# Splitting the w2t loads of the first stage in two, and waiting for each x tile by itself

## The chip, the cores and the metric

The program runs on the 8 cores of one Trainium2 chip. Each core gets 1024 of the 8192 rows of the input and all of the weights; no core talks to another. The metric is the device time of the slowest core, in microseconds.

## The reference, cut to what matters

```python
def reference(x, w1, w2, b2, sparse_mask, qweight, scales, scaled_zeros, bias):
    def attn(x):                      # D = 4096
        a = jnp.einsum('ds,td->st', w1, w2) * sparse_mask
        y = jnp.einsum('bds,st->bdt', x, a) + b2
        return gelu(y)                # exact gelu
    def ffn(x):
        w = (qweight.astype(f32) * scales + scaled_zeros).reshape(4096, 4096)
        return jnp.einsum('bsi,oi->bso', x, w) + bias
    x = x + 0.5 * ffn(layernorm(x))
    x = x + attn(layernorm(x))
    x = x + 0.5 * ffn(layernorm(x))
    return x
```

x is 8192 x 4096 in float32. The mask is a band: of 32 x 8 blocks of 128 x 512 it touches 55.

## The kernel before

There are two blocks, one after the other. **The first block** makes the weights, on each core for itself. It builds the masked product of w1 and w2 (`amat`, bf16, in DRAM) for the 55 blocks that the mask touches, and it turns the quantized weight into a transposed bf16 matrix (`wdqT`, in DRAM). **The second block** does the three layers for the core's 1024 rows, 512 rows at a time (u = 0 and 1), in three passes each (p = 0, 1, 2: ffn, attention, ffn).

In the first block the order is written out by hand. `P_PAIRS` holds 14 pairs (sb, tc): sb is one of four blocks of 1024 columns of w1 (`w1blk`, 128 x 32 x 1024 in bf16), tc one of eight blocks of 512 columns of w2 (`w2t`, two slots of 128 x 32 x 512 in bf16, slot qq % 2). A pair has 1 to 6 tiles k (`K_TILES`), 55 in all; the pairs have 6, 5, 2, 2, 5, 6, 1, 2, 6, 6, 2, 1, 6 and 5 tiles. A tile is 32 matmuls of 128 x 128 by 128 x 512 (L393, dc = 0 to 31) into one of two PSUM tiles `pa`. VectorE multiplies it by the mask (L314, `aev`), GpSimd stores it (L256, `amat`).

Where a tc comes for the first time (`TC_FIRST`, 8 pairs: 0, 1, 2, 5, 6, 9, 10, 13), GpSimd loads w2t from w2T in float32 with a cast to bf16 (L247, semaphore `wt_ld`), and ScalarE's queue writes it back as `w2b` (L348). Where a tc comes again (6 pairs: 3, 4, 7, 8, 11, 12), SP's queue loads it from `w2b` (L273, `wr_ld`). Both loads stand in their queues behind what the pair before issues: L247 comes after the last amat store of the pair before, L273 after its last mask load. Pairs 3, 7 and 11 begin a new sb: GpSimd also loads w1blk in four parts (L234), the first two counted on `w1_lda`, the last two on `w1_ldb`. TensorE waits for `w1_lda` ahead of the first matmul of such a pair and for `w1_ldb` ahead of the 17th:

```python
                            for dc in range(NC):
                                if new_sb and k == PAIR_TILES[qq][0] and dc == 16:
                                    t.wait_ge(w1_ldb, 32 * (sb + 1))
```

Between the tiles the quantized weight is worked on by fixed positions: GpSimd loads rows (`qt`, L224), VectorE dequantizes (`wout`, L302, 32 instructions a row block), TensorE transposes (L372, 32), VectorE copies out (`asm`, L326, 32), and ScalarE's queue stores (`wdqT`, L357).

In the second block a pass begins with a layer norm of four row tiles j. For the first pass ScalarE sums x (L496) and its squares (L503), VectorE forms the scale and normalizes (L616), TensorE transposes 32 blocks (L539), VectorE copies them out (L627, `hT`). When all four are through, eight groups of matmuls (L559) run on weights that SP loads (L465, L453, `mv`, two slots) and VectorE adds the result to `x_sb` (L641). After u = 0, SP stores the four tiles of `x_sb` (L474, a semaphore `st_o[j]` each) and then issues the first two mv loads of u = 1. GpSimd waits for each store and loads the next rows into the same tile:

```python
                    for j in range(NT):
                        g.wait_ge(st_o[j], 16)
                        g.dma_start(
                            out=x_sb[:, j * D:(j + 1) * D],
                            in_=x_in[512 + j * 128:512 + (j + 1) * 128, :],
                        ).then_inc(x_ld2, 16)
```

ScalarE waits ahead of its first L496 of u = 1 until `x_ld2` stands at 64, that is for all four.

Of the kernel before, what the change touches and what calls it, by code (L numbers as in the profile page):

```python
# [15 lines left out]
NC = 32  # L16
# [101 lines left out]
def build_nc():  # L118
# [47 lines left out]
    wt_ld = semn("wt_ld", 2)  # L166
    wr_ld = semn("wr_ld", 2)
    mk_ld = semn("mk_ld", 2)
    p1_st = semn("p1_st", 2)
    x_ld = sem1("x_ld")  # L170
    x_ld2 = sem1("x_ld2")
    st_o = semn("st_o", 4)
    mv_ld = semn("mv_ld", 2)

    with es:
# [7 lines left out]
        with nc.Block() as block:  # L183
            from contextlib import ExitStack as _ES

            with _ES() as es_1:
# [15 lines left out]
                def _(g):  # L202
# [25 lines left out]
                    for qq, (sb, tc) in enumerate(P_PAIRS):  # L228
# [12 lines left out]
                        if TC_FIRST[qq]:  # L241
                            if qq >= 2:
                                g.wait_ge(p1_pe, K_BEFORE[qq - 1])
                                if TC_FIRST[qq - 2]:
                                    g.wait_ge(wb_st[P_PAIRS[qq - 2][1]], 16)
                            sl2 = (qq % 2) * NC * 512
                            g.dma_start(  # L247
                                out=w2t[:, sl2:sl2 + NC * 512]
                                    .rearrange("p (c t) -> p c t", t=512),
                                in_=w2T.rearrange("(c p) t -> p c t", p=128)  # L250
                                    [:, :, tc * 512:(tc + 1) * 512],
                            ).then_inc(wt_ld[qq % 2], 16)
                        for k in PAIR_TILES[qq]:
                            Sg = K_TILES[k][3]
# [10 lines left out]
                def _(sync):  # L265
                    for qq, (sb, tc) in enumerate(P_PAIRS):
                        if not TC_FIRST[qq]:
                            sync.wait_ge(p1_pe, K_BEFORE[qq - 1])
                            if TC_FIRST[qq - 2]:
                                sync.wait_ge(wb_st[P_PAIRS[qq - 2][1]], 16)  # L270
                            sync.wait_ge(wb_st[tc], 16)
                            sl2 = (qq % 2) * NC * 512
                            sync.dma_start(  # L273
                                out=w2t[:, sl2:sl2 + NC * 512]
                                    .rearrange("p (c t) -> p c t", t=512),
                                in_=w2b.rearrange("(c p) t -> p c t", p=128)
                                    [:, :, tc * 512:(tc + 1) * 512],
                            ).then_inc(wr_ld[qq % 2], 16)
                        for k in PAIR_TILES[qq]:
                            Sg = K_TILES[k][3]  # L280
# [54 lines left out]
                def _(s):  # L335
# [6 lines left out]
                    for _, kind, idx in sorted(acts):  # L342
                        if kind == 0:
                            qq = idx
                            tc = P_PAIRS[qq][1]
                            sl2 = (qq % 2) * NC * 512
                            s.wait_ge(wt_ld[qq % 2], WT_CNT[qq])
                            s.dma_start(  # L348
                                out=w2b.rearrange("(c p) t -> p c t", p=128)
# [14 lines left out]
                def _(t):  # L364
# [12 lines left out]
                    for qq, (sb, tc) in enumerate(P_PAIRS):  # L377
# [8 lines left out]
                        for k in PAIR_TILES[qq]:  # L386
# [3 lines left out]
                            for dc in range(NC):  # L390
                                if new_sb and k == PAIR_TILES[qq][0] and dc == 16:
                                    t.wait_ge(w1_ldb, 32 * (sb + 1))
                                ins = t.matmul(  # L393
# [11 lines left out]
            with _ES() as es_2:  # L405
# [12 lines left out]
                def _(g):  # L418
                    for j in range(NT):
                        g.wait_ge(st_o[j], 16)  # L420
                        g.dma_start(
                            out=x_sb[:, j * D:(j + 1) * D],
                            in_=x_in[512 + j * 128:512 + (j + 1) * 128, :],
                        ).then_inc(x_ld2, 16)

# [57 lines left out]
                def _(s):  # L483
                    for _tc in range(8):
                        s.wait_ge(wb_st[_tc], 16)
                    for u in range(2):
                        for p in range(3):
                            for j in range(NT):
# [3 lines left out]
                                if p == 0:  # L492
                                    s.wait_ge(x_ld if u == 0 else x_ld2, 64)
                                    if u == 1:
# [183 lines left out]
```

## Time and profile before

| what | us |
|---|---|
| runs: median of 2 (lowest, highest) | 3102.33 (3054.62, 3150.04) |
| the profiled execution | 3068.76 |
| its span, slowest core (core 3) | 3067.2 |
| spans of the other cores | 3022.0 to 3050.6 |
| granted TensorE clock, mean, share of full | 0.761 to 0.768 |
| first block, to the issue of the first x load | 1377.3 |
| PE busy in the whole span | 1889.1 |
| PE L393 busy (1760 matmuls) | 458.8 |

The profiled execution is one run of its own beside the two that make the median. The span runs from the first to the last instruction of the slowest core; 1.6 us lie around it. A line such as L393 is a line of the kernel before. "Idle before" is time in which an engine stood still ahead of an instruction, and the name behind the arrow is what ended it.

### The profile page before, as it was taken

The page shows a single profiled execution, that of the slowest core. Times are in us where ns is not written, and L with a number is a line of the kernel's source. Part 1 is how long each engine was busy: PE and PEld are TensorE (multiplying, and loading weights), DVE is VectorE, ACT ScalarE, POOL GpSimd, SP SyncE. Part 2 cuts the span into 40 slices and gives each one's busy share as a digit, 9 for nine tenths or more (in the row PEclk, how much of TensorE's full clock was granted, in tenths as well). Part 3 has the DMA queues.
Part 4 walks back from the last instruction along what each step waited for, and adds up shares of the span by engine and source line. Part 5 has one row for each costly group of instructions (what it writes and reads, how often), then busy time and mean ns, then how long its engine had stood idle before and what let it go on. Part 6 is the DMA issues. An engine that isn't in the chain of part 4 may idle for free.

```text
span 3067.2 us, 25494 instructions; the slowest of 8 cores (3022.0 to 3067.2 us)
## 1 busy us (share of the span) xinstructions
PE 1889.1 (62%) x8280; PEld 845.1 (28%) x8280; DVE 757.6 (25%) x3395; ACT 168.3 (5%) x157; POOL 83.0 (3%) x124
## 2 busy tenths in 40 slices
PE   0552254721657225372999765889629997658896
PEld 0220122300223112131343322333213333224332
DVE  0032234420454224354000324100031003241000
ACT  0000000000000000004000213000040002130000
POOL 1000000000000000000000000000000000000000
PEclk9965677855778657685899776889758997668888
DMA  9688979999588996866233014144372430141342
GB/s 157 144 164 174 174 132 139 172 178 180 117 142 179 187 181 122 148 137 214 96 124 110 23 50 132 55 138 136 93 236 82 137 110 23 50 132 55 130 145 110
DMA packets 402702, 399.49 MB, mean 130 GB/s; under 512 B 135696, under 2 KB 370992, under 8 KB 396432
## 3 DMA queue, kind: packets, MB, share of 16 engines
q1 hardware_dynamic: 180240, 213.39, 23.9%
q0 software_dynamic: 57856, 117.37, 23.8%
q10 hardware_dynamic: 164480, 67.11, 9.5%
q8 instruction: 72, 1.18, 0.2%
q14 instruction: 54, 0.44, 0.1%
HBM read 407.47 MB, written 91.10 MB: 163 GB/s over the span
## 4 chain that ended last, share of the span: by engine, by line
PE 54%; another core or an unknown queue 17%; DVE 12%; DMA 8%; issue 5%; ACT 2%; DVEq 1%; POOL 0%; SPq 0%; ACTq 0%; POOLq 0%
PE ps L559 36%; PE pa L393 13%; DMA w2t<-w2T 5%; DVE x_sb L641 3%; DVE asm L326 3%; DVE hT L627 2%; PE ptr L372 2%; DVE wout L302 2%; DVE h_tmp L616 2%; PE ps L569 2%; PE tr L539 1%; DMA x_sb<-x_in 1%; DMA y_out<-x_sb 1%; ACT sq_scr L503 1%
## 5 line engine op out<-in xcount | busy, mean ns | idle before, releaser
L559 PE MATMUL ps<-mv,hT 128*128 128x512 bf16 x4536 | 1098.7, 408 | 141.9 <-DVE x_sb L641 137.4
L393 PE MATMUL pa<-w2t,w1blk 128*128 128x512 bf16 x1760 | 458.8, 428 | 702.6 <-DMA w2t<-w2T 449.8
L559 PEld LDWEIGHTS ps<-mv,hT 128*128 128x128 bf16 x4536 | 466.6, 104 | 772.2 <-issue 312.8
L393 PEld LDWEIGHTS pa<-w2t,w1blk 128*128 128x128 bf16 x1760 | 186.3, 108 | 961.7 <-issue 805.0
L641 DVE SCALAR_TENSOR_TENSOR x_sb<-ps,x_sb 128x512 f32<-128x512 f32 x128 | 80.8, 687 | 1007.0 <-PE ps L569 1007.0
L539 PE MATMUL tr<-ident_bf,h_tmp 128*128 128x128 bf16 x768 | 132.8, 264 | 257.6 <-DVE h_tmp L616 245.5
L314 DVE TENSOR_TENSOR aev<-pa,mkt 128x512 bf16<-128x512 f32 x55 | 37.9, 690 | 838.8 <-PE pa L393 838.8
L302 DVE TENSOR_SCALAR wout<-qt,scl_sb,zro_sb 128x128 bf16<-128x128 bf16 x1024 | 235.5, 325 | 0.0
L372 PE MATMUL ptr<-ident_bf,wout 128*128 128x128 bf16 x1024 | 161.2, 230 | 53.8 <-DVE asm L326 43.4
L326 DVE COPY asm<-ptr 128x128 bf16<-128x128 bf16 x1024 | 166.5, 219 | 18.2 <-PE ptr L372 3.7
L539 PEld LDWEIGHTS tr<-ident_bf,h_tmp 128*128 128x128 bf16 x768 | 80.2, 105 | 311.7 <-issue 291.7
L627 DVE COPY hT<-tr 128x128 bf16<-128x128 bf16 x768 | 125.0, 220 | 34.3 <-PE tr L539 18.5
L372 PEld LDWEIGHTS ptr<-ident_bf,wout 128*128 128x128 bf16 x1024 | 97.9, 98 | 121.6 <-issue 81.6
L503 ACT ACTIVATE sq_scr<-x_sb 128x4096 bf16<-128x4096 f32 x24 | 86.8, 3616 | 563.2 <-DVE x_sb L641 560.5
L641 DVE SCALAR_TENSOR_TENSOR x_sb<-gel,x_sb 128x512 f32<-128x512 f32 x64 | 41.8, 690 | 172.7 <-ACT gel L521 172.7
L496 ACT ACT_TABLE_LOAD x1 | 1.3, 1283 | 1406.2 <-DMA x_sb<-x_in 1406.2
L256 POOL DMA_DIRECT2D amat<-aev x55 | 30.3, 551 | 1255.3 <-DVE aev L314 887.7
L616 DVE TENSOR_SCALAR h_tmp<-x_sb,stats 128x4096 bf16<-128x4096 f32 x24 | 57.9, 2412 | 4.6 <-DVE stats L611 4.6
L496 ACT ACTIVATE sq_scr<-x_sb 128x4096 bf16<-128x4096 f32 x8 | 28.9, 3617 | 335.7 <-DMA x_sb<-x_in 334.7
L521 ACT ACTIVATE gel<-ps 128x512 f32<-128x512 f32 x64 | 36.4, 596 | 156.2 <-PE ps L569 149.1
L596 DVE TENSOR_SCALAR stats<-stats 128x1 f32<-128x1 f32 x24 | 3.6, 151 | 119.6 <-ACT sq_scr L503 118.3
L569 PE MATMUL ps<-fb_bf,halves_bf 1*128 1x512 bf16 x128 | 33.0, 377 | 0.0
(32 smaller groups left out, 134.0 us busy)
## 6 DMA issues: line engine op xcount, KB each, us to landing
mv<-wdqT SPq DMA_DIRECT2D x32, 4096.0 KB, 15.0
w1blk<-w POOLq DMA_DIRECT2D x16, 2048.0 KB, 57.3
w2t<-w2T POOLq DMA_DIRECT2D x8, 4096.0 KB, 49.4
w2b<-w2t ACTq DMA_DIRECT2D x8, 4096.0 KB, 16.9
qt<-qw POOLq DMA_DIRECT2D x32, 1024.0 KB, 12.8
wdqT<-asm ACTq DMA_DIRECT2D x32, 1024.0 KB, 11.2
w2t<-w2b SPq DMA_DIRECT2D x6, 4096.0 KB, 67.0
y_out<-x_sb SPq DMA_DIRECT2D x8, 2048.0 KB, 16.0
```

The source lines that it names most:

```text
L302: v.tensor_scalar(wout[:, sl * D + gg * 128: sl * D + gg * 128 + 128], qt[:, sl * D + gg * 128: sl * D + gg * 128 + 128], scl_sb[:, r * 32 ...
L314: v.tensor_tensor(aev[:, (k % 2) * 512:(k % 2) * 512 + 512], pa[k % 2][:], mkt[:, (k % 2) * 512:(k % 2) * 512 + 512], op=ALU.mult,).then_i ...
L326: v.tensor_copy(asm2[:, (r % 2) * D + blk * 128: (r % 2) * D + blk * 128 + 128], ptr[b % 4][:],).then_inc(wqev, 1)
L372: t.transpose(ptr[b % 4][:], wout[:, (r % 2) * D + blk * 128: (r % 2) * D + blk * 128 + 128], ident_bf[:]).then_inc(wqtr, 1)
L393: ins = t.matmul(pa[k % 2][:], w1blk[:, dc * 1024 + st * 128: dc * 1024 + st * 128 + 128], w2t[:, (qq % 2) * NC * 512 + dc * 512: (qq % 2) ...
L503: s.activation(sq_scr[:], x_sb[:, j * D:(j + 1) * D], AF.Square, accum_out=stats[:, 4 + j:5 + j]).then_inc(ac_ln, 1)
L539: t.transpose(trp[tg % 4][:], h_tmp[:, ic * 128:(ic + 1) * 128], ident_bf[:]).then_inc(p2_tr, 1)
L559: t.matmul(psb[j][:], hT[:, ic * 512 + j * 128: ic * 512 + j * 128 + 128], mv[:, sl + ii * 512:sl + ii * 512 + 512], start=(ii == 0), stop ...
L569: ins = t.matmul(psb[j][:], lrow[0:1, :], brow[0:1, oc * 512:(oc + 1) * 512], start=False, stop=True,)
L616: v.tensor_scalar(h_tmp[:], x_sb[:, j * D:(j + 1) * D], stats[:, 8 + j:9 + j], stats[:, 20 + j:21 + j], op0=ALU.subtract, op1=ALU.mult).th ...
L627: v.tensor_copy(hT[:, ic * 512 + j * 128: ic * 512 + j * 128 + 128], trp[tg % 4][:],).then_inc(p2_trv, 1)
L641: v.scalar_tensor_tensor(x_sb[:, j * D + oc * 512: j * D + oc * 512 + 512], src, 1.0, x_sb[:, j * D + oc * 512: j * D + oc * 512 + 512], o ...
```

## The change

Each of the 14 w2t loads becomes two: chunks 0 to 15 on the semaphore it had, chunks 16 to 31 on a new one (`wtb_ld` for GpSimd's loads, `wrb_ld` for SP's). TensorE waits for the second one ahead of the 17th matmul of a pair's first tile. ScalarE's queue waits for both ahead of the write-back. Apart from that the four x loads of u = 1 get a semaphore each, and ScalarE waits ahead of L496 of tile j for the load of tile j.

```diff
+    wtb_ld = semn("wtb_ld", 2)
+    wrb_ld = semn("wrb_ld", 2)
-    x_ld2 = sem1("x_ld2")
+    x_l2 = semn("x_l2", 4)
...
+                            w2Tv = w2T.rearrange("(c p) t -> p c t", p=128)
                             g.dma_start(
-                                out=w2t[:, sl2:sl2 + NC * 512]
+                                out=w2t[:, sl2:sl2 + 16 * 512]
                                     .rearrange("p (c t) -> p c t", t=512),
-                                in_=w2T.rearrange("(c p) t -> p c t", p=128)
-                                    [:, :, tc * 512:(tc + 1) * 512],
+                                in_=w2Tv[:, 0:16, tc * 512:(tc + 1) * 512],
                             ).then_inc(wt_ld[qq % 2], 16)
+                            g.dma_start(
+                                out=w2t[:, sl2 + 16 * 512:sl2 + NC * 512]
+                                    .rearrange("p (c t) -> p c t", t=512),
+                                in_=w2Tv[:, 16:NC, tc * 512:(tc + 1) * 512],
+                            ).then_inc(wtb_ld[qq % 2], 16)
...
                             s.wait_ge(wt_ld[qq % 2], WT_CNT[qq])
+                            s.wait_ge(wtb_ld[qq % 2], WT_CNT[qq])
...
                             for dc in range(NC):
-                                if new_sb and k == PAIR_TILES[qq][0] and dc == 16:
-                                    t.wait_ge(w1_ldb, 32 * (sb + 1))
+                                if k == PAIR_TILES[qq][0] and dc == 16:
+                                    if new_sb:
+                                        t.wait_ge(w1_ldb, 32 * (sb + 1))
+                                    t.wait_ge(
+                                        (wtb_ld if TC_FIRST[qq] else wrb_ld)
+                                        [qq % 2], WT_CNT[qq])
...
-                        ).then_inc(x_ld2, 16)
+                        ).then_inc(x_l2[j], 16)
...
                                 if p == 0:
-                                    s.wait_ge(x_ld if u == 0 else x_ld2, 64)
+                                    if u == 0:
+                                        s.wait_ge(x_ld, 64)
+                                    else:
+                                        s.wait_ge(x_l2[j], 16)
                                     if u == 1:
                                         s.wait_ge(p2_ev, 96)
```

SP's load from `w2b` is split in the same way, on `wr_ld` and `wrb_ld`. The tables `P_PAIRS`, `QW_AT`, `DQ_AT` and `TR_AT` are as before.

On TensorE the tiles of pair 1 stand so before (the first row is the pair's first matmul, L393):

```order
L393 MATMUL pa<-w2t,w1blk 128x512 [waits wt_ld1,p1_ev]
L393 MATMUL pa<-w2t,w1blk 128x512 x31
L393 MATMUL pa<-w2t,w1blk 128x512 [waits p1_ev]
L393 MATMUL pa<-w2t,w1blk 128x512 x31
L393 MATMUL pa<-w2t,w1blk 128x512 [waits p1_ev]
```

and so now (L410 is the same line in the changed kernel):

```order
L410 MATMUL pa<-w2t,w1blk 128x512 [waits wt_ld1,p1_ev]
L410 MATMUL pa<-w2t,w1blk 128x512 x15
L410 MATMUL pa<-w2t,w1blk 128x512 [waits wtb_ld1]
L410 MATMUL pa<-w2t,w1blk 128x512 x15
L410 MATMUL pa<-w2t,w1blk 128x512 [waits p1_ev]
```

The first tile has a second wait in its middle; the matmuls keep their order. On GpSimd's queue the load of pair 2 stood, ahead of the w1blk loads of pair 3, so:

```order
L247 DMA w2t<-w2T 128x32x512 [waits p1_pe,wb_st0]
L256 DMA amat<-aev 128x512 [waits p1_ev]
L224 DMA qt<-qw 128x4096 [waits q_dq]
L256 DMA amat<-aev 128x512 [waits p1_ev]
L234 DMA w1blk<-w 128x8x1024 [waits p1_pe]
```

and stands now so:

```order
L250 DMA w2t<-w2T 128x16x512 [waits p1_pe,wb_st0]
L255 DMA w2t<-w2T 128x16x512
L263 DMA amat<-aev 128x512 [waits p1_ev]
L226 DMA qt<-qw 128x4096 [waits q_dq]
L263 DMA amat<-aev 128x512 [waits p1_ev]
L236 DMA w1blk<-w 128x8x1024 [waits p1_pe]
```

The second half follows the first at once; nothing else has changed its place.

## Rows read from the trace of the kernel before

**Rows 1.** The page, section 4: shares of the span in the chain, by line.

```profile
PE ps L559 36%; PE pa L393 13%; DMA w2t<-w2T 5%; DVE x_sb L641 3%; DVE asm L326 3%; DVE hT L627 2%; PE ptr L372 2%; DVE wout L302 2%; DVE h_tmp L616 2%; PE ps L569 2%; PE tr L539 1%; DMA x_sb<-x_in 1%; DMA y_out<-x_sb 1%; ACT sq_scr L503 1%
```

**Rows 2.** Waits up to 1400 us: us in total, times, longest us.

```profile
PE pa L393 <- DMA w2t<-w2T: 449.8, 8, 96.3
...
PE pa L393 <- DMA w1blk<-w: 252.9, 6, 57.9
```

**Rows 3.** Timeline of PE: start us, us, what [idle before <-releaser].

```profile
96.27 43.63 PE L393 MATMUL pa<-w2t,w1blk 128*128 128x512 bf16 x192 [96.27 <-DMA w2t<-w2T]
...
299.95 9.64 PE L393 MATMUL pa<-w2t,w1blk 128*128 128x512 bf16 x32 [58.35 <-DMA w2t<-w2T]
...
386.85 5.42 PE L393 MATMUL pa<-w2t,w1blk 128*128 128x512 bf16 x16 [56.15 <-DMA w1blk<-w]
420.77 12.43 PE L393 MATMUL pa<-w2t,w1blk 128*128 128x512 bf16 x48 [28.50 <-DMA w1blk<-w]
...
546.84 9.09 PE L393 MATMUL pa<-w2t,w1blk 128*128 128x512 bf16 x32 [44.80 <-DMA w2t<-w2T]
...
791.00 6.42 PE L393 MATMUL pa<-w2t,w1blk 128*128 128x512 bf16 x16 [29.82 <-DMA w1blk<-w]
...
929.44 8.94 PE L393 MATMUL pa<-w2t,w1blk 128*128 128x512 bf16 x32 [41.78 <-DMA w2t<-w2T]
```

**Rows 4.** Timeline of POOL: three groups of load issues.

```profile
142.57 1.71 POOL L247 DMA_DIRECT2D w2t<-w2T  x1
...
326.59 3.52 POOL L234 DMA_DIRECT2D w1blk<-w  x4 [0.29 <-issue]
...
504.56 1.77 POOL L247 DMA_DIRECT2D w2t<-w2T  x1
```

**Rows 5.** The four w1blk loads issued at 326.6: issue to landing.

```profile
DMA to landing us min/median/max: 37.1/67.2/91.4
```

**Rows 6.** Windows: length, PE, PEld, DVE, ACT, POOL busy, PEclk, DMA share, GB/s.

```profile
110.00:120.00 10.00, 10.00 (x48) 4.56 (x47) 1.27 (x2) 0.00 (x0) 0.56 (x1) 1.00 0.28 80
...
300.00:310.00 10.00, 9.82 (x36) 3.89 (x36) 0.16 (x1) 0.00 (x0) 0.00 (x0) 0.74 0.97 322
320.00:330.00 10.00, 8.69 (x50) 4.56 (x48) 4.95 (x28) 0.00 (x0) 3.96 (x5) 0.95 1.06 143
...
1000.00:1010.00 10.00, 4.39 (x21) 1.77 (x19) 9.57 (x39) 0.00 (x0) 2.83 (x3) 0.92 0.59 126
```

**Rows 7.** Timeline between the halves: ACT's 1st, 2nd and 4th L496, PE's first L559.

```profile
2254.52 3.62 ACT L496 ACTIVATE sq_scr<-x_sb 128x4096 bf16<-128x4096 f32 x1 [334.65 <-DMA x_sb<-x_in]
...
2263.41 3.62 ACT L496 ACTIVATE sq_scr<-x_sb 128x4096 bf16<-128x4096 f32 x1 [0.20 <-ACT stats L509]
...
2284.73 3.62 ACT L496 ACTIVATE sq_scr<-x_sb 128x4096 bf16<-128x4096 f32 x1 [0.20 <-ACT stats L509]
...
2305.11 1.44 PE L559 MATMUL ps<-mv,hT 128*128 128x512 bf16 x3 [0.69 <-DVE hT L627]
```

**Rows 8.** Line L421, first of its four loads: issue and landing.

```profile
L421 POOL DMA_DIRECT2D x_sb<-x_in x1: 542/542/542, 2208.6 to 2208.6; - x1
...
DMA to landing us min/median/max: 20.4/20.4/20.4
```

**Rows 9.** Line L421, second of its four loads.

```profile
L421 POOL DMA_DIRECT2D x_sb<-x_in x1: 539/539/539, 2217.6 to 2217.6; - x1
...
DMA to landing us min/median/max: 21.7/21.7/21.7
```

**Rows 10.** DMA issues of SP at 2203: KB each, us to landing.

```profile
mv<-wdqT SPq DMA_DIRECT2D x1, 4096.0 KB, 66.7
```

**Rows 11.** Core 2, the same place: first load of L421, first L496.

```profile
L421 POOL DMA_DIRECT2D x_sb<-x_in x1: 539/539/539, 2199.4 to 2199.4; - x1
...
DMA to landing us min/median/max: 20.3/20.3/20.3
...
2248.91 3.62 ACT L496 ACTIVATE sq_scr<-x_sb 128x4096 bf16<-128x4096 f32 x1 [335.85 <-DMA x_sb<-x_in]
```

More of the change, by code:

```diff
@@ L272, in _ @@
                             sl2 = (qq % 2) * NC * 512
+                            w2bv = w2b.rearrange("(c p) t -> p c t", p=128)
                             sync.dma_start(
-                                out=w2t[:, sl2:sl2 + NC * 512]
+                                out=w2t[:, sl2:sl2 + 16 * 512]
                                     .rearrange("p (c t) -> p c t", t=512),
-                                in_=w2b.rearrange("(c p) t -> p c t", p=128)
-                                    [:, :, tc * 512:(tc + 1) * 512],
+                                in_=w2bv[:, 0:16, tc * 512:(tc + 1) * 512],
                             ).then_inc(wr_ld[qq % 2], 16)
+                            sync.dma_start(
+                                out=w2t[:, sl2 + 16 * 512:sl2 + NC * 512]
+                                    .rearrange("p (c t) -> p c t", t=512),
+                                in_=w2bv[:, 16:NC, tc * 512:(tc + 1) * 512],
+                            ).then_inc(wrb_ld[qq % 2], 16)
                         for k in PAIR_TILES[qq]:
```

## Prediction

> **What bounds the kernel now.** I read the page's chain first. Its largest part is the second block's matmuls, L559 with 36%, which the change does not touch; w2t loads stand in it with 5%, and the two transfers of x between the halves with about 1% each [rows 1]. So the change can only work at two places, and I looked at each.
>
> The first is the first block. The table of waits up to 1400 us says that TensorE stood 449.8 us for a w2t load from w2T, in 8 waits, and 252.9 us for w1blk, in 6 [rows 2]. Eight is the number of pairs with a new tc; the six others are the two waits each of pairs 3, 7 and 11. No wait for a load from w2b is in the table: the six loads of SP are never late. The timeline of TensorE shows the pattern: a stand of 41 to 58 us, then a first tile of 32 matmuls in 8.9 to 9.6 us [rows 3]. GpSimd issues such a load only when the pair before is through, at 142.57 for pair 1 and 504.56 for pair 5 [rows 4], and pair 5 starts 42.3 us after its issue, at 546.84. So load and computation follow one another and do not overlap, and what shortens the computation behind a landing brings the next issue forward.
>
> The second place lies between the halves. The first x load is issued at 2208.6 and lands 20.4 us later [rows 8]; ScalarE's first L496 starts at 2254.52 and is said to wait for an x load [rows 7], though the tile that it reads has been there for 25 us. It waits for all four.
>
> **The w2t loads, eight pairs.** Take a load that lands at T. Before, 32 matmuls of the first tile stand behind T; now 16, since the first 16 run when the first half has landed. For this the halves must land one after the other with at least the time of 16 matmuls between. The four w1blk loads show that they do: they are issued within 3.5 us on the same queue [rows 4], the earliest lands after 37.1 us and the latest after 91.4 [rows 5], and TensorE began on the first two at 386.85 and on the last two at 420.77 [rows 3]. Two of four had landed after 60 of 94 us, or 64%. The same share of a 42 us load is 27 us, which leaves 15 us; 16 matmuls after a stand take 5.42 [rows 3]. They fit.
>
> What is gained is not these 5.42. After the second wait the array is slow again: the 48 matmuls from 420.77 take 12.43 us, although 16 had run 28.5 us earlier, while 192 in a row take 43.63, or 0.227 each [rows 3]. So the slow start is paid twice, and what is saved is 32 matmuls after a stand (9.64, 9.09, 8.94; mean 9.22) less 16 after a stand (5.42; once 6.42). That is 3.8, or 2.8 by the slower row; 16 matmuls at 0.227 are 3.6. I take 3.7, with 2.8 and 4.2 as ends (9.64 less 5.42).
>
> The Trainium skill has the rule behind this (TensorE: Matmul & The Clock Gate, "What's actually happening"): an idle array falls back to 1.2 GHz, so work put ahead of an idle stretch warms nothing behind it. The trace agrees, with 5.42 us for 16 after a stand against 3.6 in a long run. Without that rule one would book 9.22 less 3.6, 5.6 a pair.
>
> How much of 3.7 reaches the end depends on what the DMA engines do behind the landing. In long pairs they run dry before the next issue: their share is 0.28 at 110 us, 0.59 at 1000 us [rows 6]. There the next load starts earlier, and all of it counts: pairs 0, 1, 5, 9 and 13, 5 x 3.7 = 18.5. Pairs 2, 6 and 10 have only 1 or 2 tiles, and the next wait is for w1blk, issued at 326.59 behind pair 2 [rows 4]. From the landing at 299.95 to that issue the engines are full, with shares of 0.97 and 1.06 [rows 6]: write-back, wdqT stores and weight rows are on their way. An issue 3.7 us earlier takes bandwidth from those, and they then take it back. The gain lies between 0 and 3.7; for something under half the bandwidth I take 1.5, 3 x 1.5 = 4.5.
>
> Twice the issues cost GpSimd nothing: four w1blk issues take 3.52 us, 0.88 each, and a whole w2t issue 1.71 to 1.77 [rows 4]; two halves make the same. SP's split loads are not waited for now, and the same bytes move in the same order, so they cost nothing unless halves move slower (below). ScalarE's write-back waits for both halves, which is when it was issued before. The evictions, dequantization and transposes of a pair keep their order and shift with the first tile.
>
> **The x tiles.** ScalarE can begin at 2208.6 + 20.4 = 2229.0 instead of 2254.5: 25.4 us, with the 0.1 of a semaphore taken off. From there to TensorE's first L559 it took 50.6 us (2254.52 to 2305.11) [rows 7], and this is work of four engines that the loads only have to feed in time. The second load lands at 2217.6 + 21.7 = 2239.3 [rows 9]; ScalarE would want it at 2263.41 less 25.4, 2238.0, so it is 1.3 late. The fourth is wanted at 2284.73 less 25.4 = 2259.3, and all have landed by 2254.5 [rows 7]. The 1.3 counts in full if ScalarE sets the pace and not at all if VectorE does; I take 0.5, which leaves 24.9. Next comes the first mv load: issued at 2203 it lands after 66.7 us [rows 10], at 2269.7, and is wanted at 2305.1 less 25.4 = 2279.7. It has 10 us to spare, so it covers nothing. On core 2 the same gap is 2199.4 + 20.3 to 2248.9 [rows 11], 29.2 us, the upper end; with 1.3 lost and a landing 4 us later than here, 20 is the lower.
>
> **The sum.** 18.5 + 4.5 + 24.9 = 47.9 us. The profiled execution took 3068.8 (span 3067.2 and 1.6 around it), so 3020.9, or 1.6% less; I say 3021. The two other runs stand at 3054.6 and 3150.0, with a median of 3102.3 that lies between two far ends; the profiled one is near the lower, and the forecast is for such an execution. A measurement of this kernel can tell about 2% from no change, and the forecast lies inside that.
>
> **The rivals.**
> 1. The DMA engines give more back. Pairs 2, 6 and 10 bring nothing, and the long pairs lose some too, since qt loads and wdqT stores are paced by computation and pile up when it is shorter. For: shares near 1 after a landing. Against: 0.28 and 0.59 before the next issue [rows 6]. With 2 us a long pair: 10 + 24.9 = 35, so 3034.
> 2. The split does not do what it says: both halves land within a few us, since each of the engines finishes at its own time. Then TensorE waits as before, and only the x tiles count: 3044. Against it stand the w1blk landings [rows 5].
> 3. Slower: halves move at a lower rate than the whole. Place: the 449.8 + 252.9 = 702.7 us in which TensorE waits for loads [rows 2]. Each 1% of rate costs 7.0 us; from 6.8% on the whole gain is gone, and at 10% it is 3068.8 - 47.9 + 70.3 = 3091. For it: nothing in the trace shows this load in halves. Against: w1blk is loaded in quarters already, with the engines at 1.06 in the window of its issue [rows 6].
> 4. More: each of the eight gives 4.2 and the x tiles 29.2 as on core 2. 33.6 + 29.2 = 62.8, so 3006, just over 2%.
>
> The Trainium skill (DMA: Bandwidth & Descriptors, "Anatomy of one DMA") gives each DMA a fixed cost of about 2.0 us, mostly the wait for the write's receipt. If the eight awaited loads each paid it once more, that would be an estimate of 16 us and 3037. No row here isolates it, and the second half is queued before the first has ended, so I leave it out.
>
> **How the numbers follow.** The forecast gets 0.58, rival 1 0.13, rival 2 0.08, rival 3 0.07, rival 4 0.14. The range goes down to rival 4 on an execution like the fastest (3006 less the 14.1 by which 3054.6 lies under 3068.8, about 2992), rounded to 2990. Upward it takes in rivals 1 and 2 with the same scatter above 3044 and the lower third of rival 3: 3068. Faster by over 2% needs 3007 or less against 3068.8: rival 4 and the scatter below the forecast, 0.27. Slower by over 2% needs rival 3 with 16% less rate, 0.04. Within 2%: 0.69.
>
> **What would show it.** L410 (the old L393) must show eight pairs of waits, the first ended by a w2t load some 15 us before the second, with 16 matmuls of about 5.4 us between. The w2t waits in all must fall from 449.8 by less than the early matmuls; from the issue of pair 5 to its second landing must stay 42 us. The first block must end near 1354 instead of 1377. ScalarE's first L496 must begin 20 us after the first x load's issue, with L559 51 us behind. I am wrong if the second half lands later than the whole did, if the w1blk waits grow by more than 3.7 us a pair, or if mv becomes the wait ahead of L559.

## The result, and the profile after

The changed kernel is faster. Its median is 2988.2 us (2977.7 to 3005.9, 11 runs), beside 3058.4 us for before in the same measurement, and the ratio is 0.9777 with a 95% interval of 0.9749 to 0.9806. Measured twice more (c1 and c3 below) the ratio is 0.9834 (0.9797 to 0.9871) and 0.9873 (0.9807 to 0.9939). The forecast was 3021 us, or 1.6% less; measured are 2.2%, 1.7% and 1.3%. Whether it is "faster by over 2%" or "within 2%" stays undecided: the first interval lies almost wholly below 0.98, the second almost wholly and the third wholly above. Executions in which one die ran at a lower clock are left out of the ratios.

The page of the changed kernel is taken on core 4. Line L410 is the old L393, L438 the old L421, L516 the old L496. The waits up to 1400 us, us in total, times, longest:

```profile
PE pa L410 <- DMA w2t<-w2T: 384.0, 16, 87.5
...
PE pa L410 <- DMA w1blk<-w: 248.4, 6, 52.7
```

The waits for w2T are 16 instead of 8, as they must be, and 384 us instead of 450 [rows 2]; those for w1blk have hardly moved. Where a pair starts is seen in the timeline of TensorE, for pair 5 (start us, us, what, idle before):

```profile
509.85 6.35 PE L410 MATMUL pa<-w2t,w1blk 128*128 128x512 bf16 x16 [26.29 <-DMA w2t<-w2T]
523.11 1.01 PE L410 MATMUL pa<-w2t,w1blk 128*128 128x512 bf16 x2 [6.91 <-DMA w2t<-w2T]
524.34 5.31 PE L410 MATMUL pa<-w2t,w1blk 128*128 128x512 bf16 x13 [0.22 <-issue]
```

and in that of GpSimd, the two issues of the same load:

```profile
486.09 1.21 POOL L250 DMA_DIRECT2D w2t<-w2T  x1
487.29 1.17 POOL L255 DMA_DIRECT2D w2t<-w2T  x1
```

The first half lands 23.8 us after its issue, the second 13.3 us behind it; between them 16 matmuls take 6.35 us and TensorE stands for 6.91. Behind the second landing 16 matmuls are left (one has no record), and they take 6.5 us: the slow start is paid again. Before, this place read 9.09 for 32 [rows 3].

Between the halves of the rows, in the timeline of core 4:

```profile
2151.18 0.54 POOL L438 DMA_DIRECT2D x_sb<-x_in  x1 [835.90 <-DMA y_out<-x_sb]
...
2173.73 3.62 ACT L516 ACTIVATE sq_scr<-x_sb 128x4096 bf16<-128x4096 f32 x1 [309.86 <-DMA x_sb<-x_in]
...
2184.38 3.62 ACT L516 ACTIVATE sq_scr<-x_sb 128x4096 bf16<-128x4096 f32 x1 [1.97 <-DMA x_sb<-x_in]
...
2204.14 3.62 ACT L516 ACTIVATE sq_scr<-x_sb 128x4096 bf16<-128x4096 f32 x1 [0.48 <-ACT stats L529]
...
2224.30 11.08 PE L579 MATMUL ps<-mv,hT 128*128 128x512 bf16 x40 [1.07 <-DVE hT L647]
```

ScalarE starts 22.6 us after the first issue, where it was 45.9 [rows 7, 8]. The second tile's load is late by 1.97 us, as forecast (1.3), and TensorE's first L579 stands 50.6 us behind ScalarE's start, to the tenth as before. On this core the lateness was hidden by the rest of the chain; on the others that distance is 50.4 to 51.6 us now, where it was 50.4 to 50.8. The first mv load landed after 67.0 us, 10 us ahead of its use.

### The profile page after: what moved, and what is told of

The parts are those of the page before. It is cut to its first block, busy times and chain, and to the rows that moved or that the text cites. A ratio compares the mean times of both kernels' runs of the same rounds, so it can differ in the third digit from the quotient of the medians.

```text
span 2990.9 us, 25381 instructions; the slowest of 8 cores (2958.5 to 2990.9 us)
## 1 busy us (share of the span) xinstructions
PE 1887.0 (63%) x8131; PEld 847.9 (28%) x8280; DVE 754.0 (25%) x3395; ACT 168.4 (6%) x157; POOL 88.4 (3%) x132
## 3 DMA queue, kind: packets, MB, share of 16 engines
q0 software_dynamic: 57984, 117.37, 24.9%
## 4 chain that ended last, share of the span: by engine, by line
PE 54%; DMA 13%; DVE 13%; another core or an unknown queue 10%; issue 6%; ACT 2%; DVEq 1%; POOL 0%; ACTq 0%; SPq 0%; POOLq 0%
PE ps L579 36%; PE pa L410 13%; DMA w2t<-w2T 9%; DVE asm L338 3%; DVE x_sb L661 3%; DVE hT L647 2%; DVE wout L314 2%; PE tr L559 2%; DVE h_tmp L636 2%; DMA x_sb<-x_in 2%; DMA w1blk<-w 2%; PE ps L589 2%; PE ptr L385 1%; ACT sq_scr L523 1%
## 5 line engine op out<-in xcount | busy, mean ns | idle before, releaser
L579 PE MATMUL ps<-mv,hT 128*128 128x512 bf16 x4438 | 1085.6, 407 | 150.8 <-DVE x_sb L661 137.1
L410 PE MATMUL pa<-w2t,w1blk 128*128 128x512 bf16 x1709 | 470.6, 440 | 641.5 <-DMA w2t<-w2T 384.0
L579 PEld LDWEIGHTS ps<-mv,hT 128*128 128x128 bf16 x4536 | 465.8, 103 | 768.8 <-issue 306.8
L410 PEld LDWEIGHTS pa<-w2t,w1blk 128*128 128x128 bf16 x1760 | 190.8, 110 | 909.7 <-issue 767.4
L559 PE MATMUL tr<-ident_bf,h_tmp 128*128 128x128 bf16 x768 | 131.6, 265 | 231.3 <-DVE h_tmp L636 218.4
L385 PE MATMUL ptr<-ident_bf,wout 128*128 128x128 bf16 x1024 | 159.8, 228 | 54.4 <-DVE asm L338 43.6
L559 PEld LDWEIGHTS tr<-ident_bf,h_tmp 128*128 128x128 bf16 x768 | 79.8, 104 | 284.6 <-issue 265.3
L516 ACT ACTIVATE sq_scr<-x_sb 128x4096 bf16<-128x4096 f32 x8 | 28.9, 3617 | 313.0 <-DMA x_sb<-x_in 311.8
L438 POOL DMA_DIRECT2D x_sb<-x_in x4 | 2.4, 594 | 867.7 <-DMA y_out<-x_sb 867.7
```

The lines of the kernel that those rows point to most:

```text
L385: t.transpose(ptr[b % 4][:], wout[:, (r % 2) * D + blk * 128: (r % 2) * D + blk * 128 + 128], ident_bf[:]).then_inc(wqtr, 1)
L410: ins = t.matmul(pa[k % 2][:], w1blk[:, dc * 1024 + st * 128: dc * 1024 + st * 128 + 128], w2t[:, (qq % 2) * NC * 512 + dc * 512: (qq % 2) ...
L559: t.transpose(trp[tg % 4][:], h_tmp[:, ic * 128:(ic + 1) * 128], ident_bf[:]).then_inc(p2_tr, 1)
L579: t.matmul(psb[j][:], hT[:, ic * 512 + j * 128: ic * 512 + j * 128 + 128], mv[:, sl + ii * 512:sl + ii * 512 + 512], start=(ii == 0), stop ...
```

## The experiments

Twelve runs were made, in four series; each series has its own runs of before beside it, on the same chip (one chip for e1 to e8, c1 and c2, another for e9 and c3; for the first measurement the chip is not on record). The ratios rest on 4 to 11 executions of the run, that of e6 on two. To read the first block I took two spans from the timelines of GpSimd and TensorE for each of its 11 load-bound stretches (the eight w2T loads and the w1blk loads of pairs 3, 7 and 11), as means over the 8 cores: from the load's issue to TensorE's last start on it ("to the landing"), and from there to the next such issue ("computation"). The first stretch begins at 0. They add up to the issue of the first x load.

| run | ratio (95%) | landings, sum | computation, sum | first x load | second block |
|---|---|---|---|---|---|
| before, first trace | | 694.8 | 660.0 | 1354.9 | 1687.1 |
| changed, first trace | 0.9777 (0.9749 to 0.9806) | 681.1 | 635.0 | 1316.1 | 1661.2 |
| e1 x tiles only | 0.9929 (0.9885 to 0.9972) | 672.6 | 663.5 | 1336.1 | 1649.8 |
| e2 w2t loads only | 0.9925 (0.9876 to 0.9975) | 668.5 | 638.1 | 1306.6 | 1686.4 |
| e3 both halves awaited | 1.0027 (0.9991 to 1.0062) | 672.7 | 667.7 | 1340.4 | 1683.6 |
| e4 SP's loads whole | 0.9945 (0.9904 to 0.9986) | 677.2 | 651.7 | 1328.9 | 1682.7 |
| c1 changed, again | 0.9834 (0.9797 to 0.9871) | 673.4 | 636.7 | 1310.1 | 1647.2 |
| c2 before, again | 0.9994 (0.9969 to 1.0020) | 671.7 | 663.3 | 1335.0 | 1678.4 |
| e5 pieces of 24 and 8 | 0.9744 (0.9710 to 0.9778) | | | 1283.5 | 1656.1 |
| e6 loads ahead, whole | 0.9585 (0.9544 to 0.9626) | | | | |
| e7 filled stand | 0.9796 (0.9745 to 0.9847) | | | 1299.5 | |
| e8 loads ahead, half | 0.9589 (0.9516 to 0.9662) | | | | 1656.9 |
| c3 changed, third time | 0.9873 (0.9807 to 0.9939) | 668.3 | 637.2 | 1305.5 | 1654.8 |

The second block is the span less the first x load's issue. A block's mean over the cores is steadier than the slowest core, but it is one execution each.

**What had to be explained.** Comparing the two first traces, the first block was 39 us shorter, not 23, and 13.7 of it came from loads that landed sooner. The prediction has no such term. Is it the split, or the execution?

**e1_x_only**: the kernel before with this edit alone.

```diff
-                        ).then_inc(x_ld2, 16)
+                        ).then_inc(x_l2[j], 16)
...
-                                    s.wait_ge(x_ld if u == 0 else x_ld2, 64)
+                                    if u == 0:
+                                        s.wait_ge(x_ld, 64)
+                                    else:
+                                        s.wait_ge(x_l2[j], 16)
```

> Only the four semaphores of the x loads, the w2t loads whole as before. My step: 25 us less between the halves (a ratio of 0.992), and a first block as long as before (first x load issued on average over the cores at 1355 us). Rival, that part of the extra gain sits behind the first block: more than 35 us less.

Measured: 0.9929, 22 us. It fits the 25, and its interval reaches from 8 to 35 us. The rival, over 35, is out. What was not expected is the first block: 1336 instead of 1355 us, though nothing in it is changed.

**e2_w2_only**: the changed kernel with the edit of e1 taken back.

```diff
-                        ).then_inc(x_l2[j], 16)
+                        ).then_inc(x_ld2, 16)
...
-                                    if u == 0:
-                                        s.wait_ge(x_ld, 64)
-                                    else:
-                                        s.wait_ge(x_l2[j], 16)
+                                    s.wait_ge(x_ld if u == 0 else x_ld2, 64)
```

> Only the split w2t loads, x tiles awaited together as before. The whole change gave 0.978, some 68 us; if the two parts add up, this one gives 40 to 45 us (0.986), of which 25 are matmuls that run ahead of the second landing and 14 are landings that come sooner. By the sum of the prediction it would be 23 us (0.9925).

Measured: 0.9925, 23 us, on the number of the prediction and below the 40 that the first comparison had led me to expect. Against e1's trace the computation is 25.4 us shorter and the landings are 4.1. The interval, 8 to 38 us, leaves out the 40 to 45 and does not part 23 from 30.

**e3_no_early**: e2 with the early start taken out.

```diff
                         if TC_FIRST[qq]:
                             t.wait_ge(wt_ld[qq % 2], WT_CNT[qq])
+                            t.wait_ge(wtb_ld[qq % 2], WT_CNT[qq])
                         else:
                             t.wait_ge(wr_ld[qq % 2], WT_CNT[qq])
+                            t.wait_ge(wrb_ld[qq % 2], WT_CNT[qq])
...
-                                if k == PAIR_TILES[qq][0] and dc == 16:
-                                    if new_sb:
-                                        t.wait_ge(w1_ldb, 32 * (sb + 1))
-                                    t.wait_ge(
-                                        (wtb_ld if TC_FIRST[qq] else wrb_ld)
-                                        [qq % 2], WT_CNT[qq])
+                                if new_sb and k == PAIR_TILES[qq][0] and dc == 16:
+                                    t.wait_ge(w1_ldb, 32 * (sb + 1))
```

> All w2t loads split, x tiles awaited together as before, but TensorE waits for both halves ahead of the first matmul, so nothing runs ahead. Theory A, that a load in two pieces lands sooner as a whole by itself: about 14 us less than before (0.995), with the mean time from the issue of a w2T load to TensorE's start near 38 us for pairs 1, 5, 9 and 13. Theory B, that the landings come sooner only because less other traffic is left once the matmuls are ahead: no gain, within 5 us of before, and that time stays near 40 to 43 us.

Measured: 1.0027. The landings of pairs 1, 5, 9 and 13 came after 38.4, 37.2, 37.7 and 37.0 us, as theory A says, but the kernel gained nothing, and e1, with whole loads, has 38.6, 37.4, 37.6 and 36.3. So neither theory holds: the landings are at 36 to 39 us in every trace of this series, whole or split. It also prices the split itself: 14 more transfers, with nothing started early, cost between nothing and 19 us by the interval, and the landings' sum differs from e1's by 0.1 us.

**e4_sp_whole**: e2 with SP's load in one piece.

```diff
-                            sync.dma_start(
-                                out=w2t[:, sl2:sl2 + 16 * 512]
...
-                            ).then_inc(wr_ld[qq % 2], 16)
-                            sync.dma_start(
-                                out=w2t[:, sl2 + 16 * 512:sl2 + NC * 512]
...
-                            ).then_inc(wrb_ld[qq % 2], 16)
+                            sync.dma_start(
+                                out=w2t[:, sl2:sl2 + NC * 512]
...
+                            ).then_inc(wr_ld[qq % 2], 16)
...
-                                    t.wait_ge(
-                                        (wtb_ld if TC_FIRST[qq] else wrb_ld)
-                                        [qq % 2], WT_CNT[qq])
+                                    if TC_FIRST[qq]:
+                                        t.wait_ge(wtb_ld[qq % 2], WT_CNT[qq])
```

> GpSimd's w2T loads split, SP's loads from w2b whole again, x tiles awaited together as before. Theory A1, that what lands sooner is GpSimd's own load because it is cut: as e2, 40 to 45 us less than before. Theory A2, that it is the cut of SP's loads, which share the DMA engines with pairs 2, 6, 10 and with w1blk: 10 us or more short of e2. By the prediction SP's cut is worth nothing.

Measured: 0.9945, 17 us, with an interval (4 to 29 us) that covers e2's 23. SP's cut is worth nothing that these runs can show. In the trace the computation is 13.6 us longer than e2's, but its cores had a lower granted clock, 0.750 to 0.767 in the mean of the span where e2's had 0.759 to 0.772. Pair 0, which no load of SP can touch, shows it: on cores 0 to 3 its computation took 48.8 to 49.7 us (granted 0.81 from 110 to 140 us on core 0), on cores 4 to 7 42.0 to 43.3 us (1.00 on core 4), where e2 has 42.1 to 43.6 on all eight. So the 13.6 us cannot be put down to SP's cut.

**c1_after and c2_before**: the two kernels themselves, unedited, on one chip.

> The changed kernel again, on a chip on which the two parts are run too. If the parts add up, 0.985 to 0.986 (0.9929 times 0.9925), 44 us, which is close to the forecast. If whole and parts differ for a reason of their own (the parts help each other), 0.978 as at first, 68 us.

> The kernel before as a control, for its trace. On the first trace of before the w2T loads of pairs 1, 5, 9, 13 took 43, 40, 39 and 39 us on average over the cores to TensorE's start, in the run with whole loads (e1) 39, 37, 38 and 36. If that is a matter of the execution and not of the split, this control gives 36 to 40 and a ratio of 1.000; if the first trace is typical of whole loads, it gives 39 to 43.

Measured: 0.9834 for the changed kernel, 0.9994 for before. The product of e1 and e2 is 0.9855, inside c1's interval: the parts add up. And the control settles the question: before has its landings at 38.4, 37.1, 37.5 and 36.9 us for pairs 1, 5, 9 and 13, where its first trace had 43.1, 39.9, 38.9 and 39.4. So the 13.7 us are not the split. They belong to the execution that the first page happened to show, or to its chip; the two cannot be told apart here. The waits of the control's slowest core:

```profile
PE pa L393 <- DMA w2t<-w2T: 421.1, 8, 95.8
...
PE pa L393 <- DMA w1blk<-w: 242.6, 6, 55.4
```

That is 29 us less for w2T than in [rows 2], for the same kernel. Beside it stands c1, with the same columns:

```profile
PE pa L410 <- DMA w2t<-w2T: 369.2, 16, 79.8
...
PE pa L410 <- DMA w1blk<-w: 243.7, 6, 51.2
```

c1 against c2 is the clean comparison: landings +1.7 us, computation -26.6, second block -31.2.

**e5_split24**: the changed kernel with another cut.

```diff
-                                out=w2t[:, sl2:sl2 + 16 * 512]
+                                out=w2t[:, sl2:sl2 + 24 * 512]
...
-                                if k == PAIR_TILES[qq][0] and dc == 16:
-                                    if new_sb:
-                                        t.wait_ge(w1_ldb, 32 * (sb + 1))
+                                if new_sb and k == PAIR_TILES[qq][0] and dc == 16:
+                                    t.wait_ge(w1_ldb, 32 * (sb + 1))
+                                if k == PAIR_TILES[qq][0] and dc == 24:
                                     t.wait_ge(
```

> The changed kernel with pieces of 24 and 8 chunks instead of 16 and 16. My step: what counts is the number of matmuls left behind the last landing. 8 left instead of 16, all in the slow stretch behind a stand, save another 2 to 3 us in each of eight pairs: 16 to 24 us under the changed kernel (0.992 to 0.995 of it), if the last piece still lands behind the first 24 matmuls. Rival, the early matmuls of 24 end behind the landing of the last 8 chunks, so TensorE is the one that is late: at most 8 us under the changed kernel.

Measured: 0.9744, which is 0.991 of c1, 27 us: above the 16 to 24 expected and far above the rival's 8. The first block is 26.6 us shorter than c1's (1283.5 to 1310.1), and 18 of them lie in the eight w2T stretches: about 2.3 us each, as expected. The rest lies around the w1blk loads and I cannot attribute it. TensorE no longer stops between the pieces. The rows of pair 5 on core 4: TensorE's timeline, the issue and landing of the second piece, and two windows, up to its landing and from there on (length, then as in [rows 6]):

```profile
503.92 9.72 PE L410 MATMUL pa<-w2t,w1blk 128*128 128x512 bf16 x31 [36.64 <-DMA w2t<-w2T]
...
L255 POOL DMA_DIRECT2D w2t<-w2T x1: 901/901/901, 471.3 to 471.3; - x1
...
DMA to landing us min/median/max: 37.4/37.4/37.4
...
503.92:508.70 4.78, 4.78 (x12) 1.71 (x13) 0.00 (x0) 0.00 (x0) 0.00 (x0) 0.50 0.52 86
508.70:513.64 4.94, 4.89 (x24) 2.19 (x24) 0.00 (x0) 0.00 (x0) 0.00 (x0) 0.94 0.83 234
```

The second piece lands at 508.7, when TensorE has started 12 of the first 24 matmuls, and the 24th ends at about 511.9. Over all 64 such loads the second piece landed 5.4 us behind the first in the mean, and the 24th matmul ended some 2 us after that (from 0.4 before to 3.7 after). So the condition of the rival came true, TensorE is the late one, but not its price: without a second stand the slow start is paid once, here at a granted clock of 0.50 at first and 0.94 behind. By these rows a still larger first piece would only start TensorE later. One somewhat smaller than 24 might do better; it was not tried.

**e7_fill**: the changed kernel, busy in the stand between the halves.

```diff
+                junk = es_1.enter_context(nc.psum_tensor("junk", [128, 512], F32))
...
                                 if k == PAIR_TILES[qq][0] and dc == 16:
+                                    if TC_FIRST[qq]:
+                                        for _f in range(24):
+                                            t.matmul(junk[:], w1blk[:, 0:128],
+                                                     w1blk[:, 0:512],
+                                                     start=True, stop=True)
                                     if new_sb:
```

> The changed kernel with 24 more matmuls (w1blk by w1blk, into a PSUM tile that nobody reads) between the early 16 and the wait for the second half, in the eight pairs with a w2T load. My step, that the slow start is paid a second time behind the stand between the halves: with TensorE busy for 5 of the 7 us of that stand, the 16 matmuls behind it take 3.5 to 4 us instead of 5 to 6.4, and the first block ends 8 to 14 us sooner than the changed kernel's. Rival, what follows the landing is not set by the clock: 16 matmuls still take over 5 us, and the kernel is as long as the changed one or, where the filling ends behind the landing, longer by up to 10 us.

Measured: 0.9796. Three of the eight places in the timeline of TensorE, core 7:

```profile
264.96 6.38 PE L416 MATMUL pa<-w2t,w1blk 128*128 128x512 bf16 x16 [43.12 <-DMA w2t<-w2T]
271.18 5.34 PE L408 MATMUL junk<-w1blk 128*128 128x512 bf16 x24
279.60 5.30 PE L416 MATMUL pa<-w2t,w1blk 128*128 128x512 bf16 x16 [3.08 <-DMA w2t<-w2T]
...
648.94 5.30 PE L416 MATMUL pa<-w2t,w1blk 128*128 128x512 bf16 x16 [2.44 <-DMA w2t<-w2T]
...
886.13 3.61 PE L416 MATMUL pa<-w2t,w1blk 128*128 128x512 bf16 x16 [1.10 <-DMA w2t<-w2T]
```

Where only 1.1 us of the stand was left, the 16 matmuls took 3.61 us; where 2.4 or 3.1 were left, 5.30. The windows of the last two say that the clock makes the difference (columns as in [rows 6]; the granted clock is the third from the end):

```profile
648.94:654.24 5.30, 5.30 (x19) 2.15 (x20) 0.00 (x0) 0.00 (x0) 0.00 (x0) 0.68 0.86 288
886.13:889.74 3.61, 3.61 (x19) 1.72 (x20) 0.00 (x0) 0.00 (x0) 0.00 (x0) 1.00 0.79 261
```

The eight cores have 64 such places. In 34 the 16 matmuls took 3.6 to 3.8 us at a granted clock of 1.00; in 22 they took 5.1 to 6.5 us at 0.54 to 0.70 in the mean, after stands of 2.3 to 7.2 us; in the other 8 they took 4.4 us at 0.81. In c1, without filling, the 16 behind the second landing take 5.7 us in the mean (4.9 to 6.5). That is the slow start switched off and on in one execution, by matmuls of the same shape, and it shows the step of the prediction. The first block is 10.6 us shorter than c1's, inside the 8 to 14. Against c1 the ratios alone (0.9796, 0.9834) decide nothing; their intervals overlap.

**e6_prefetch**: the changed kernel with the whole load moved a pair ahead.

```diff
+                    def w2_part(q2, part):
+                        tc2 = P_PAIRS[q2][1]
+                        o2 = (q2 % 2) * NC * 512 + part * 8 * 512
+                        g.dma_start(
...
+                        ).then_inc((wt_ld if part < 2 else wtb_ld)[q2 % 2], 16)
...
+                        if qq + 1 < NP and TC_FIRST[qq + 1] and qq >= 1:
+                            g.wait_ge(p1_pe, K_BEFORE[qq])
+                            if TC_FIRST[qq - 1]:
+                                g.wait_ge(wb_st[P_PAIRS[qq - 1][1]], 16)
                         for k in PAIR_TILES[qq]:
+                            part = k - PAIR_TILES[qq][0]
+                            if qq + 1 < NP and TC_FIRST[qq + 1] and part < 4:
+                                w2_part(qq + 1, part)
                             g.wait_ge(p1_ev, k + 1)
```

> The changed kernel with each w2T load in four pieces, one issued ahead of each of the first four amat stores of the pair before, so that it runs beside the computation. Theory P, that the stands for w2T are there only because the load is issued late: seven of the eight stands of 38 us go, and the DMA engines, idle in a part of the long pairs, take the load there; 100 to 200 us less than the changed kernel. Rival, the DMA engines are full anyway: the loads push the qt loads, wdqT stores and amat stores back, VectorE waits instead, and less than 50 us are gained.

Measured: 0.9585, from two executions, 126 us less than before and 76 less than c1. That is between the two theories.

**e9_prefetch_again**: the kernel of e6, unedited.

> The kernel of e6 again, for a second trace and a second ratio. If the trade seen in e6 is the kernel's own, VectorE waits 150 to 200 us for wdqT stores, these land after a median near 50 us, and the ratio is 0.954 to 0.963. If it was that execution's, the wait is under 100 us and the ratio lower.

One execution came out of it that can be compared, 2925.9 us, beside a fastest of 3030.8 for before (0.965), so there is no new interval. I read core 2, the slowest of cores 0 to 3. The waits up to 1400 us show both theories at work:

```profile
PE ptr L388 <- DVE asm L341: 242.4, 42, 40.0
DVE asm L341 <- DMA wdqT<-asm: 174.4, 6, 34.0
PE pa L414 <- DMA w2t<-w2T: 116.2, 3, 85.5
```

Of c1's 369 us for w2T 116 are left, 86 of them the first load, which has nothing to run beside. In their place VectorE waits 174 us in six waits for wdqT stores, and TensorE waits for VectorE. Where the w2T loads are not issued ahead, these stores land in time: here is the table of DMA issues (KB each, median us to landing) of core 2 in c3, and then in e9:

```profile
w2b<-w2t ACTq DMA_DIRECT2D x8, 4096.0 KB, 27.3
...
wdqT<-asm ACTq DMA_DIRECT2D x32, 1024.0 KB, 9.8
```

```profile
w2b<-w2t ACTq DMA_DIRECT2D x8, 4096.0 KB, 56.8
...
wdqT<-asm ACTq DMA_DIRECT2D x32, 1024.0 KB, 43.6
```

The expectation for the wait (150 to 200 us) is met; cores 0 and 1 have 166 and 157 us. That for the landing (near 50) is met roughly at best: core 2 has the highest median of its four, the cores 0, 1 and 3 have 38.4, 29.5 and 35.7 us, beside 9.8 to 10.2 on cores 0 to 3 of c3.

**e8_half_ahead**: e6 with two of the four pieces ahead, late in the pair, and two at the pair's begin.

```diff
+                        if TC_FIRST[qq]:
+                            w2_part(qq, 2)
+                            w2_part(qq, 3)
...
-                            part = k - PAIR_TILES[qq][0]
-                            if qq + 1 < NP and TC_FIRST[qq + 1] and part < 4:
+                            part = k - PAIR_TILES[qq][-1] + 1
+                            if qq + 1 < NP and TC_FIRST[qq + 1] and part >= 0:
                                 w2_part(qq + 1, part)
```

> The changed kernel with the w2T load in four pieces: the first two are issued ahead of the last two amat stores of the pair before, the other two when the pair begins, with waits ahead of matmuls 1, 17 and 25. With all four ahead (e6) the wdqT stores that run beside them landed after a median of 50 instead of 10 us and VectorE waited 183 us for them. Theory: the price falls on stores that are in flight with a load, so pieces issued late in a pair meet fewer of them, and most of the stand still goes: at least as good as e6, 0.945 to 0.96 of before. Rival, the same bytes meet the same stores wherever they stand: between the split into 24 and 8 and e6, 0.96 to 0.974.

Measured: 0.9589 (0.9516 to 0.9662), the same as e6. The stall of VectorE is gone from the table of waits, TensorE stands again for w2T (core 3):

```profile
PE pa L422 <- DMA w2t<-w2T: 315.9, 23, 90.1
PE pa L422 <- DMA w1blk<-w: 224.0, 6, 48.4
```

The wdqT stores still take a median of 30.2 us here, but nothing waits for them. So one wait was traded for the other, and the sum came out alike. I had expected the later pieces to be at least as good, which they are, and by the interval not shown to be better. Both kernels beat before and the changed kernel; e6 and e8 cannot be told apart.

**c3_after**: the changed kernel, unedited, in the series of e9.

> The changed kernel a third time. The two ratios so far are 0.9777 and 0.9834, the product of the parts 0.9855. If the forecast of 48 us is the right size and the first measurement was high, 0.983 to 0.986; if something of 20 us is missing from the sum, 0.975 to 0.979.

Measured: 0.9873, 39 us, with 0.9807 to 0.9939. The ratio lies above both ranges; the interval takes in the first and leaves out the second. It fits the forecast's size and speaks against 20 us missing from the sum. Its first block ends at 1305.5 us, 4.6 before c1's.

## Why the prediction came out as it did

**The time.** Forecast 47.9 us less. Measured are 68 us at first, 51 in c1 and 39 in c3, so 53 in the mean of the three; the parts alone give 22 and 23. The mechanism was right in both parts, with one term of the sum too small (below). The first median, 2988.2 us, lies 2 us under the low end of the stated range, 2990. Part of that is the base: the before measured with it stood at 3058.4 and not at 3068.8. On that scale the forecast would read 3011, and on the forecast's own, 0.9777 of 3068.8 is 3000. Why the first measurement gave some 20 us more than the two later ones is open: its interval overlaps c1's by 0.0009 and misses c3's, and no run shows a cause. From c2 to c1 the first block falls by 24.9 us in the mean over the cores, where 23.0 was forecast.

**Five long pairs, 18.5 us.** Right. From c2 to c1 the computation of pairs 0, 1, 5, 9 and 13 falls by 3.5, 3.9, 3.8, 3.3 and 2.8 us, 17.3 in all, or 3.5 a pair against 3.7.

**Three short pairs, 4.5 us.** This step of the sum was mis-sized. The prediction said that w1blk, issued 3.7 us earlier, "takes bandwidth from those, and they then take it back", and booked 1.5 of 3.7. From c2 to c1 the computation of pairs 2, 6 and 10 falls by 2.9, 3.6 and 3.1 us, and the three w1blk stretches behind them change by -1.4, -0.8 and +3.3. So 9.6 less 1.1, 8.5 us, stayed. More traces say the same: the computation of the three short pairs is 63.1 to 64.3 us in the four traces without an early start (the two of before, e1, e3) and 53.4 to 53.9 in the five with one (the three of the changed kernel, e2, e4), and the three w1blk stretches sum to 269.5 us in the mean of the four and to 268.5 in that of the five. So about 10 us came, and nothing was taken back that these traces show. A DMA share of 0.97 and 1.06 [rows 6] was read as a sign that most of an earlier issue is lost, but it moved the landing of w1blk forward in full. The share says that the engines are busy, not for whom; why w1blk keeps its place among the other transfers was not tried.

**The second start is slow again.** Right, and it is what kept the estimate from 5.6 a pair. e7 shows it by itself: 3.61 us at a granted clock of 1.00 with 1.1 us of stand, 5.30 at 0.68 with 2.4.

**Halves land one after the other.** Right: 13 us apart for pair 5 where 15 was forecast. Rival 2 is out. Rival 3, a lower rate in halves, is out by c1 and c2: the landings' sums are 673.4 and 671.7 us.

**Issues and SP's split cost nothing.** Right within what e3 and e4 can tell. The half issues take 1.2 us each and not 0.88, so a load costs GpSimd 2.4 instead of 1.7 us; it is seen in no wait. The estimate by the Trainium skill (DMA: Bandwidth & Descriptors, "Anatomy of one DMA"), 2 us more for each awaited transfer and 16 in all, did not come in the traces: the landings' sums of c1 and c2 differ by 1.7 us, those of e3 and e1 by 0.1. The times alone do not exclude it, as e3's interval reaches to 19 us.

**The x tiles, 24.9 us.** Right. From c2 to c1 the time from the first x issue to ScalarE's start falls from 45.2 to 18.5 us on average over the cores, 26.7, and TensorE follows 50.8 instead of 50.6 us later. Over all traces, 40 cores with the x tiles awaited together (the two of before, e2, e3, e4) and 56 with each by itself (e1, e5, e7, e8 and the three of the changed kernel), the first falls from 46.4 to 19.0 us and the second rises from 50.4 to 50.9. So the lateness of the second tile costs the 0.5 us that was booked, and 26.9 us are left. mv never became the wait: it lands 5 to 14 us ahead of its use on all cores of the changed kernel's traces.

**What the base was.** The prediction named the scatter of executions and took the first trace as it was. That trace had 23 us more in its landings than the control, on a chip that may be another one, which shifted the comparison of traces though not the ratio.

## What to carry to other kernels

When a wait is split, count the instructions that remain behind the last landing and price them at the rate that the engine has after a stand, not the instructions that were started early. A cut that leaves no second stand avoids the second slow start: 24 of 32 was better than 16 here, though TensorE was then some 2 us behind the last landing in the mean, so the best cut may lie between. Before a term is built on the difference of two traces, take a second trace of the same kernel: here one load stretch differed by up to 5 us between two executions of unchanged code (perhaps on two chips). And a load that is awaited because it is issued late is worth moving before it is worth cutting: 76 us more than the split alone gave came from issuing it one pair ahead (there in four pieces; a whole load ahead was not tried), although the DMA engines were then near full and the wdqT stores took three to four times as long.

## What the runs showed of the hardware

- A stand of 1.1 us left TensorE's 16 matmuls at 3.61 us (granted clock 1.00), one of 2.4 us was followed by 5.30 (0.68). In both places 24 filling matmuls had run in 5.34 us, 0.22 each, right before (e7, core 7).
- With w2T loads of GpSimd in flight beside them, the 1 MB stores of wdqT took a median of 44 instead of 9.8 us, and the 4 MB stores of w2b 57 instead of 27.3 (core 2; on cores 0, 1 and 3 wdqT took 30 to 38 and w2b 41 to 55), while the mean DMA share of the first 1280 us rose only from 0.89 to 0.95 (windows of core 2, c3 and e9, below; the share is the last but one). Which property of the stores makes them give way was not tried.

```profile
0.00:1280.00 1280.00, 621.74 (x2764) 284.67 (x2764) 429.39 (x2084) 0.00 (x0) 85.97 (x128) 0.74 0.89 168
```

```profile
0.00:1280.00 1280.00, 601.70 (x2784) 283.38 (x2784) 430.72 (x2107) 0.00 (x0) 96.02 (x144) 0.73 0.95 176
```

- GpSimd issues 8 chunks of a w2T load in 0.90 us and 24 in 1.50 (e5), 16 in 1.17 to 1.21, all 32 in 1.71 to 1.77 [rows 4]. So the issue has a part that does not shrink with the size: 0.6 us, an estimate from the rows of 8, 16 and 24 chunks, which rise by 0.3 us for each 8.
- An issue 3 us earlier into DMA engines with a share of 0.97 and 1.06 [rows 6] was not lost: the three w1blk stretches did not grow (268.5 us against 269.5).
